# Self attention's heads in sets of four: four products side by side in one PSUM bank

## What is computed

```python
qkv = h @ w_qkv
q, k, v = jnp.split(qkv, 3, axis=-1)          # reshaped to (B, S, H, hd)
scores = jnp.einsum('bqhd,bkhd->bhqk', q, k) * hd ** (-0.5)
scores = jnp.where(causal, scores, jnp.finfo(scores.dtype).min)
attn = jax.nn.softmax(scores, axis=-1)
o = jnp.einsum('bhqk,bkhd->bqhd', attn, v).reshape(B, S, D)
x_resid = x + o @ w_o
```

## Time and profile before

| | us |
|---|---|
| median of three runs (3508.27 to 3514.3) | 3511.59 |
| profiled execution, its own time | 3526.84 |
| its span, first to last instruction | 3524.6 |
| self attention, from the first maximum tile to the last head's end | 593.0 |
| PE busy in the span | 2867.8 |
| DVE, ACT, POOL busy in the span | 2089.9, 1436.8, 1370.2 |

### The profile page before, as it was taken

One profiled execution on the slowest core, in us unless ns is written; L12 is line 12 of the kernel. 1 busy time (PEld: TensorE's weight loads), 2 busy tenths in 40 slices (PEclk: granted clock), 3 DMA queues, 4 the chain that ended last, 5 costly groups with the idle time before them and its releaser, 6 DMA issues. The chain is left out here.

```text
span 3524.6 us, 30222 instructions
## 1 busy us (share of the span) xinstructions
PE 2867.8 (81%) x8560; PEld 1248.7 (35%) x8560; DVE 2089.9 (59%) x2977; ACT 1436.8 (41%) x2168; POOL 1370.2 (39%) x1138
## 2 busy tenths in 40 slices
PE   5888988888775877999999829999478887779966
PEld 1232332333222543222222228888132332226522
DVE  1899999999995436444444230000339999932233
ACT  4566556655643322333333302221246555422233
POOL 2588788778774012000000140000437788720010
PEclk8999999999998978999999959999589999986688
DMA  1222022012200002100100224444221022000000
GB/s 62 94 96 93 26 96 102 32 71 96 79 18 18 1 14 90 28 19 20 26 18 19 69 97 142 179 180 142 79 96 63 35 96 96 0 18 0 0 7 24
DMA packets 67914, 215.28 MB, mean 61 GB/s; under 512 B 15517, under 2 KB 40361, under 8 KB 48697
## 3 DMA queue, kind: packets, MB, share of 16 engines
q1 hardware_dynamic: 61384, 181.12, 14.4%
q10 hardware_dynamic: 3312, 24.12, 2.0%
q0 software_dynamic: 3072, 8.39, 0.7%
HBM read 187.97 MB, written 25.43 MB: 61 GB/s over the span
## 5 line engine op out<-in xcount | busy, mean ns | idle before, releaser
L750 POOL TENSOR_TENSOR s_dbu<-s_dx,s_bc 128x512 f32<-128x512 f32 x768 | 975.0, 1275 | 313.3 <-DVE s_psum L490 312.3
L420 PE MATMUL s_psum<-s_hc,ident 128*128 128x512 f32 x1536 | 850.2, 638 | 209.9 <-DVE s_hc L506 209.1
L639 ACT ACTIVATE s_psum<-s_dt,s_a_neg 128x512 f32<-128x512 f32 x768 | 526.5, 690 | 631.0 <-DVE s_hc L506 630.2
L506 DVE TENSOR_TENSOR s_hc<-s_psum,s_bc 128x512 f32<-128x512 f32 x768 | 519.5, 677 | 0.9 <-issue 0.6
L420 PEld LDWEIGHTS s_psum<-s_hc,ident 128*128 128x128 f32 x1536 | 240.0, 190 | 764.4 <-DVE s_hc L506 686.0
L490 DVE TENSOR_TENSOR_SCAN s_psum<-s_psum,s_state,s_dbu 128x512 f32<-128x512 f32 x384 | 490.5, 1277 | 10.2 <-ACT s_psum L639 10.2
L490 DVE TENSOR_TENSOR_SCAN s_psum<-s_psum,s_dbu 128x512 f32<-128x512 f32 x384 | 468.5, 1220 | 12.8 <-ACT s_psum L639 9.9
L1329 DVE TENSOR_REDUCE s_umax<-s_banks 128x1 f32<-128x512 f32 (+3 forms) x384 | 210.3, 554 | 282.6 <-PE s_banks L1195 223.5
L1233 PE MATMUL s_banks<-s_probs,s_vs 128*17 128x512 f32 (+3 forms) x768 | 324.4, 512 | 35.6 <-ACT s_ot L1410 32.3
L1419 ACT ACTIVATE s_probs<-s_banks 128x512 f32<-128x512 f32 (+3 forms) x384 | 187.3, 489 | 395.7 <-PE s_banks L1219 295.5
L1780 ACT ACTIVATE s_hidden<-s_banks,s_w 128x256 f32<-128x256 f32 x184 | 77.1, 470 | 302.8 <-PE s_banks L1603 302.8
(11 more groups left out here) (249 smaller groups left out, 3626.0 us busy)
## 6 DMA issues: line engine op xcount, KB each, us to landing
s_bc<-fwd_rows SPq DMA_DIRECT2D x64, 1024.0 KB, 4.8
s_bc<-m_rows SPq DMA_DIRECT2D x32, 1024.0 KB, 4.7
s_w<-in_moe_w SPq DMA_DIRECT2D x23, 1028.0 KB, 7.3
s_w<-in_moe_w ACTq DMA_DIRECT2D x23, 1024.0 KB, 5.6
s_stack<-qk_parts SPq DMA_DIRECT2D x192, 64.0 KB, 2.1
qk_parts<-s_parts SPq DMA_DIRECT2D x48, 128.0 KB, 1.8
moe_in_rows<-s_zero SPq DMA_DIRECT2D x1, 5888.0 KB, 19.1
s_xs<-moe_in_rows SPq DMA_DIRECT2D x23, 256.0 KB, 6.0
```

The source lines that it names most:

```text
L420: pe.matmul(psum[:, SCANS + block_no % 2, :], consts["ident"][:], hc[:, unit % PRODUCTS, :], start=(n == 0), stop=(n == NS - 1)).then_inc( ...
L506: dve.tensor_tensor(hc[:, unit % PRODUCTS, :], psum[:, unit % SCANS, :], bc[:, 2 * n + 1, :], ALU.mult)\
L639: act.activation(psum[:, unit % SCANS, :], dt[:, g % 2, i // NS, :], ACT.Exp, scale=a_neg[CHUNKS[g][0]][:, i:i + 1]).then_inc(decay_ready, 1)
L750: pool.tensor_tensor(dbu[:, unit % TERMS, :], dx[:, g % 2, i // NS, :], bc[:, 2 * n, :], ALU.mult)\
```

## The change

Heads are handled in sets of four of one batch, eight sets `q`, with all loops written out.

- The value product has weights of 32 columns (`VW`: 16 channels, the ones column, 15 columns of zeros). The four heads of a set write partitions 0, 32, 64 and 96 onwards of one bank, one after another in PE's list (`mix_heads`), straight from `v`; the copy `vs` by POOL goes. One semaphore increment per four.
- Outputs and maxima are transposed per set: four 128x128 transposes per half (`turn_out`), one transpose of 32 columns (`turn_max`), one row split for 32 partitions, three row DMAs per set. `copy_out` copies 128 partitions. All transposes use bank 6.
- PE's order: per unit four weight tiles, each followed by a maximum tile of the next set, and a fifth maximum tile (`MAX_STEP`), then the four products of the unit before. Set q + 1's maxima are done in set q's units 0 to 9 and turned in unit 10. Weights have three banks (2, 3, 7), maxima two.
- `stack` becomes `stack_q` and `stack_k` with three slots of four heads of one batch. A set's 12 DMAs are 128 KB each, in rows of 1024 elements; three sets are loaded ahead, the next when the set three back has its last weights.
- The whole of `v`'s columns 16 to 31 is cleared, then the ones are written, and `stack_k`'s ones cover 3 x 12288 elements.

The diff, cut: of functions that are replaced only the new lines and what they keep are shown; `store_row` has the same four steps as before, on 32 partitions; `misc` numbers the users of bank 6 in order.

```diff
 PARTS = 3
 QPARTS, KPARTS = (0, 0, 0, 1, 1, 2), (0, 1, 2, 0, 1, 0)
 STACK = len(QPARTS) * HD
-VW = HD + 1
+VW = 32
+SLOTS = 3
+WEIGHT_BANKS = (2, 3, 7)
...
-        vs = s.sb("vs", [P, B * QT, HH, VW])
-        stack = s.sb("stack", [STACK + PARTS, HH, 2, T], BF16)
-        umax = s.sb("umax", [P, 2, 12])
-        row = s.sb("row", [QT, 2, PARTS, P], BF16)
-        row_rest = s.sb("row_rest", [QT, P])
-        probs = s.sb("probs", [P, 4, CH])
-        ot = s.sb("ot", [VW, 2, S])
-        rden = s.sb("rden", [P, 2, QT, 1])
+        stack_q = s.sb("stack_q", [STACK + PARTS, SLOTS, HH, S], BF16)
+        stack_k = s.sb("stack_k", [STACK + PARTS, SLOTS, HH, S], BF16)
+        umax = s.sb("umax", [P, 2, HH, QT])
+        late_max = s.sb("late_max", [P, 2, HH, QT // 2])
+        row = s.sb("row", [HH * QT, 2, PARTS, P], BF16)
+        row_rest = s.sb("row_rest", [HH * QT, P])
+        probs = s.sb("probs", [P, 2 * HH, CH])
+        ot = s.sb("ot", [P, 2, CH])
+        rden = s.sb("rden", [P, 2, QT // 2, HH, 1])
...
         NU = len(UNITS)
-        NN = HH * B
-        NTURN = H // HH
+        NSETS = H // HH * B
+        TILES = NU * HH
+        MAX_STEP = 5
...
             for stored in parts_stored:
                 sp.wait_ge(stored, NCH // 2 * STORES)
+            sp.wait_ge(made, 4)
+            def load_set(q):
+                g, b = q // B, q % B
+                if q >= SLOTS:
+                    sp.wait_ge(scored, (q - SLOTS + 1) * TILES)
+                for which, stack, order in ((0, stack_q, QPARTS), (1, stack_k, KPARTS)):
                     for r, part in enumerate(order):
+                        sp.dma_start(stack[r * HD:(r + 1) * HD, q % SLOTS, :, :],
+                                     qk_d[which, part, g * HH:(g + 1) * HH, :, b * S:(b + 1) * S]
+                                     .rearrange("h e t -> e h t")).then_inc(stack_ready[q % SLOTS], 16)
+            def store_rows(q):
+                sp.wait_ge(row_ready, q + 1)
+                for part in range(PARTS):
+                    sp.dma_start(stack_q[STACK + part:STACK + part + 1, q % SLOTS, :, :],
+                                 row[:, q % 2, part, :]).then_inc(row_stored[q % 2], 16)
+            for q in range(SLOTS):
+                load_set(q)
+            store_rows(0)
+            for q in range(NSETS):
+                if q + 1 < NSETS:
+                    store_rows(q + 1)
+                if q + SLOTS < NSETS:
+                    load_set(q + SLOTS)
         @block.tensor
         def _(pe):
...
             pe.wait_ge(split2, 4 + NCH * 4)
+            pe.wait_ge(made, 4)
+            def max_tile(q, k):
+                u, j = k // HH, k % HH
+                t, half = MAX_UNITS[u]
+                i = q * TILES + k
+                if k == 0:
+                    pe.wait_ge(stack_ready[q % SLOTS], (q // SLOTS + 1) * (12 * 16))
+                if i >= 2:
+                    pe.wait_ge(max_read, i - 1)
+                w = min((t + 1) * P - half * CH, CH)
+                bank = banks[:, i % 2, :]
+                mm = pe.matmul(bank[:, 0:w], stack_q[0:STACK, q % SLOTS, j, t * P:(t + 1) * P],
+                               stack_k[0:STACK, q % SLOTS, j, half * CH:half * CH + w], start=True, stop=True)
+                if t // 4 == half:
+                    mm = pe.matmul(bank[:, w - P:w], consts["identb"][:], lateb[:, 0, :], start=False,
+                                   stop=True, skip_group_check=True)
+                mm.then_inc(max_ready, 1)
+            def turn_max(q):
+                pe.wait_ge(maxed, q + 1)
+                if q:
+                    pe.wait_ge(misc_read, misc["max", q])
+                pe.transpose(banks[0:HH * QT, 6, 0:P], umax[:, q % 2, :, :].rearrange("p j t -> p (j t)"),
+                             consts["ident"][:]).then_inc(turned, 1)
+            def weight_tile(q, u, j):
+                t, half = UNITS[u]
+                i = q * TILES + u * HH + j
+                if u == 0 and j == 0:
+                    pe.wait_ge(row_stored[q % 2], (q // 2 + 1) * (PARTS * 16))
+                if i >= len(WEIGHT_BANKS):
+                    pe.wait_ge(exp_done, i - len(WEIGHT_BANKS) + 1)
+                q0 = max(t * P, half * CH)
+                w = (half + 1) * CH - q0
+                bank = banks[:, WEIGHT_BANKS[i % len(WEIGHT_BANKS)], :]
+                mm = pe.matmul(bank[:, 0:w], stack_k[:, q % SLOTS, j, t * P:(t + 1) * P],
+                               stack_q[:, q % SLOTS, j, q0:q0 + w], start=True, stop=True)
+                if t // 4 == half:
+                    mm = pe.matmul(bank[:, 0:P], consts["identb"][:], lateb[:, 1, :], start=False, stop=True,
+                                   skip_group_check=True)
+                mm.then_inc(scored, 1)
+            def mix_heads(q, u):
+                g, b = q // B, q % B
+                t, half = UNITS[u]
+                if q and t == 0:
+                    pe.wait_ge(ot_copied, 2 * (q - 1) + half + 1)
+                pe.wait_ge(exp_done, q * TILES + (u + 1) * HH)
+                w = (half + 1) * CH - max(t * P, half * CH)
+                for j in range(HH):
+                    mm = pe.matmul(banks[j * VW:(j + 1) * VW, 4 + half, CH - w:CH], v[:, b * QT + t, g * HH + j, :],
+                                   probs[:, u % 2 * HH + j, 0:w], start=(t == 0), stop=(t == 4 * half + 3))
+                mm.then_inc(pv_done, 1)
+            def turn_out(q, half):
+                pe.wait_ge(ot_copied, 2 * q + half + 1)
+                pe.wait_ge(misc_read, misc["out", q, half])
+                for t in range(QT // 2):
+                    mm = pe.transpose(banks[:, 6, t * P:(t + 1) * P], ot[:, half, t * P:(t + 1) * P], consts["ident"][:])
+                mm.then_inc(o_ready, 1)
+            for k in range(TILES):
+                max_tile(0, k)
+            turn_max(0)
+            for q in range(NSETS):
+                for u in range(NU):
+                    for j in range(HH):
+                        weight_tile(q, u, j)
+                        if q + 1 < NSETS and u * MAX_STEP + j < TILES:
+                            max_tile(q + 1, u * MAX_STEP + j)
+                    if q + 1 < NSETS and u * MAX_STEP + HH < TILES:
+                        max_tile(q + 1, u * MAX_STEP + HH)
+                    if u:
+                        mix_heads(q, u - 1)
+                    if q and u == 2:
+                        turn_out(q - 1, 1)
+                    if u == 7:
+                        turn_out(q, 0)
+                    if q + 1 < NSETS and u == 10:
+                        turn_max(q + 1)
+                mix_heads(q, NU - 1)
+            turn_out(NSETS - 1, 1)
+            pe.wait_ge(misc_read, len(misc))
...
         @block.vector
         def _(dve):
-            for sem in (max_read, row_ready, normed):
-                dve.sem_inc(sem, 1)
             dve.sem_inc(split2, 4)
             dve.sem_inc(out_free, 4)
-            dve.memset(v[:, :, :, HD:VW], 1.0).then_inc(made, 1)
-            dve.memset(stack[STACK:STACK + PARTS, :, 1, :], 1.0).then_inc(made, 1)
+            dve.memset(v[:, :, :, HD:VW], 0.0).then_inc(made, 1)
+            dve.wait_ge(made, 1)
+            dve.memset(v[:, :, :, HD:HD + 1], 1.0).then_inc(made, 1)
+            dve.memset(stack_k[STACK:STACK + PARTS, :, :, :], 1.0).then_inc(made, 1)
...
+            def maxima(q, k):
+                u, j = k // HH, k % HH
+                t, half = MAX_UNITS[u]
+                i = q * TILES + k
+                w = min((t + 1) * P - half * CH, CH)
+                to = umax[:, q % 2, j, t:t + 1] if half == 0 else late_max[:, q % 2, j, t - 4:t - 3]
+                dve.wait_ge(max_ready, i + 1)
+                dve.tensor_reduce(to, banks[:, i % 2, 0:w], AX.X, ALU.max).then_inc(max_read, 1)
+            def finish_max(q):
+                dve.wait_ge(max_read, (q + 1) * TILES)
+                dve.tensor_tensor(umax[:, q % 2, :, 4:8], umax[:, q % 2, :, 4:8], late_max[:, q % 2, :, :], ALU.max)\
+                   .then_inc(maxed, 1)
+            def store_row(q):
+                dve.wait_ge(turned, q + 1)
+                if q >= 2:
+                    dve.wait_ge(row_stored[q % 2], q // 2 * (PARTS * 16))
+                low = banks[0:HH * QT, 6, 0:P]
...
+            def norm_heads(q, half):
+                g, b = q // B, q % B
+                m = banks[:, 6, :].rearrange("p (t j e) -> p t j e", t=QT // 2, j=HH)
+                dve.wait_ge(o_ready, 2 * q + half + 1)
+                dve.reciprocal(rden[:, half], m[:, :, :, HD:HD + 1]).then_inc(rden_ready, 1)
+                dve.wait_ge(rden_ready, 2 * q + half + 1)
+                t0 = b * QT + half * QT // 2
+                dve.tensor_tensor(on[:, t0:t0 + QT // 2, g * HH:(g + 1) * HH, :], m[:, :, :, 0:HD],
+                                  rden[:, half].to_broadcast([P, QT // 2, HH, HD]), ALU.mult).then_inc(misc_read, 1)
+            for k in range(TILES):
+                maxima(0, k)
```

(63 more changed lines are left out.)

201 lines of the change are left out of this document (21 added, 180 removed).

## The result

The changed kernel takes 3292.68 us (median of 4 runs, 3291.57 to 3298.22), the kernel before beside it on the same chip 3510.43 us. The profiled execution takes 3291.57 us, its span is 3289.6.

What follows compares the result with a forecast made beforehand. TensorE was the bound, value products its largest part. (33.8 + 7 x 55.5 + 41) x 1.012 = 469 us for 593: 124 saved, less 7.8 setup, 2 loads, 8 clock: 106, median 3405 us; range 3305 to 3490.

Steps and rivals of the forecast that it cites:

- Products in four strips: Value products on TensorE: a group of four takes five stream lengths, 2.15 us plus 0.15 for loads; 21.2 us per set.
- a0 b0 a1 b1: Assumed TensorE order in a group: a and b are a product's two passes; b0 waits for a0, a1 may run beside b0.
- Rival B: Value products overlap fully, b0 not blocking a1: two streams per group, set 44, part 374, total 3310 us; chance 0.16.
- Rival A: Strips do not run side by side: eight passes in turn, set 65.6, part 551, total 3480 us; chance 0.20.
- The factor of 1.012: Correction to the laid-out part with heads: the layout gave 586 us for the kernel before's 593.0.
- Rivals C and D: C: TensorE's clock at its lower level throughout, 3621 us, chance 0.09. D: no net change, Rival A with strip drains, 0.05.
- Changes of mode: TensorE switching between bf16 tiles and value products: 12 per set instead of 48, 2.3 us for 9.1.
- Maxima: Five maximum tiles per unit, two DVE banks: TensorE newly waits for reduces, 0.92 us per full unit, some 6.5 per set.
- Row at the edge: TensorE idles 2.5 to 3 us at each of 7 set edges, waiting for the next set's maximum row.
- Prologue: Before the sets: 48 maximum tiles paced by DVE, 28 us, plus the uncovered row chain, 5.9: 33.8 us, previously 17.80.
- Setup: DVE's clearing of v and larger ones for stack_k, ahead of its first split: 7.8 us more, not covered.
- Loads: First set's 12 transfers of 128 KB instead of 64 KB before the first tile: 2 us more (0 to 6).

Runs made afterwards that it cites:

- the kernel with two strips: Against the changed kernel, the first two products of a group write the first strip, the last two the second: 3337.27 us, ratio 0.9516 to the kernel before.
- the first experiment: Against the changed kernel, all four products of a group write the first strip, so none run side by side: 3448.12 us, ratio 0.9826 to the kernel before.
- the spread kernel: Against the changed kernel, the four products keep their strips but stand apart, one after each head's weights and maxima: 3460.68 us, ratio 0.9860 to the kernel before.

## Why the prediction was wrong

**The bound of the kernel before** was read rightly: products with the values, on TensorE, were what could be gained.

**Products in four strips: the step that failed.** The text put it so: "TensorE starts matmuls in program order", so "b0 must wait for a0, a1 may run beside b0", five streams, 2.15 us and 0.15 for loads. Measured: two streams and 1.00 us. A product that waits for its own strip does not hold back one for another strip, as the kernel with two strips shows (1.85 us for 4 streams). The order a0 b0 a1 b1 was an inference from rows in which all matmuls used the same columns; they could not tell blocking from mere order. How the wait is resolved inside, by a queue for each strip or by an order other than I assumed, the traces leave open. The eight records of a group start as four and four, 0.45 us apart, and name no strip. Per set, the groups take 6 x 1.00 and, by the start differences of the narrower ones (0.78, 0.57 and 0.36 us for 384, 256 and 128 columns, twice each), 3.4 us for the other six: 9.4 in all, where 21.2 were set. That is 11.8 us per set, 94 us of the part.

The Trainium skill states both sides. "TensorEngine Tiling (Array Packing)", Key Properties, has tiles that work independently, and this case's group of 1.00 us agrees. "TensorE: Matmul & The Clock Gate", Part 3, has matmuls that start and end strictly in program order; the group with two strips disagrees, if its products reach TensorE in the order of the program, because there the third product did not wait for the second. The same Part 3 has 2.38 for three column strips; the four strips here gave 3.55.

**Rival B** was this case, with 0.16. It gave a group of 1.05, a set of 44 and a part of 374 us; measured are 1.00, 42.0 and 359.8. Its 3310 is 17 us above the result. **Rival A** was built as the first experiment: set 65.6, part 551 and 3480 forecast, 61.6, 517.4 and 3448 measured. Both were too long in the same direction. For A the mis-sized term is the clock: the layout gave 62.6 at full clock, I spread 0.93 over it, and 0.99 was granted. The factor of 1.012 and the last set's 52 carry the rest. **Rivals C and D** are excluded: the clock of the main stretch is 0.94, and changing strips costs nothing that can be seen (1.00 us for four products, 0.98 for one).

**Changes of mode.** A product alone takes 0.98 us for 0.86 of streams, and about 0.09 more stands before it in the spread kernel, where 0.19 per pair was set: the size holds. It was no lever: of 55 us of changes saved, 45 were eaten by waits for VectorE and ScalarE.

**Maxima.** 6.5 us of waits per set were forecast. From start to start it is 37 us in seven sets, 5.2 each, so the term holds. "ACT isn't late" nearly holds too: 10 us over all sets. **Row at the edge:** 2.5 to 3 us forecast, 2.7 measured. The clock behind it was set at 1 us per edge and measured 2.4. **Prologue:** 33.8 forecast, 35.0 measured. **ACT's pause** of 34 us went, as said.

**Setup:** 7.8 us forecast; VectorE's first split moved from 8.8 to 18.1 us behind the first matmul, 9.3. The zeros took 3.47 for my 4.3, but a gap of 2.62 us came before the last memset. **Loads:** 2 us forecast (0 to 6), 6.9 measured: 14.5 us from first issue to first tile for 7.6 (5.2 to 7.1 over all kernels with this load). I had taken the issue as the pace (0.49 a transfer), but the transfers themselves are slower. A set of four heads is 1.57 MB, which alone needs 14.3 us, 110 GB/s; before, half the bytes in a quarter of the packets (192 of 4 KB, now 768 of 2 KB) took 7.6. The time went with the bytes and not with the packets, though no run changes one alone. So the first maximum tile came 17 us later, not 10.

**The sum.** Part 469 forecast and 359.8 measured, 109 us more saved: seven sets of 42.0 for 55.5 are 95 us, the last set with 30.7 for 41 is 10, the factor of 1.012 is 5, and the prologue takes 1 back. The text gives 55.5 for a set of 53.8 at a clock of 0.93 without the working; the 41 us of weights, maxima and groups would by themselves grow by 3.1. Setup and loads took 16 us for 10. The 8 us put aside for the clock are already inside the measured part. 106 + 109 + 8 - 6 = 217, for 218.

## What to carry to other kernels

When a trace shows a resource used in one way only, order of starts is no evidence of blocking: keep the case of full overlap at more than a small chance, and price it first, because it is the largest. When the busiest engine gets much faster, look for what it will now wait for: here a short chain of about 6 us at each set's edge cost its own wait of 2.7 us and 2.4 us of clock. Moving it three units ahead, with the maxima spread evenly, gave 50 us of 3293. Idle time of the weight loads' queue is no measure of such a cost; the distance from start to start on TensorE is. Work that must be done before the first link of a chain (fills, constants) belongs on an engine that is idle later.

## What the runs showed of the hardware

- Four fp32 products in four strips of 32 columns: 1.00 us for 512 columns, against 3.55 on one strip and 0.98 for one product alone. Three products more cost 0.02 us.
- A product waiting for its strip does not delay one for another strip: 1.85 us for two and two, if they come in the program's order. Two products of one strip wrote the same PSUM addresses in all runs here, so whether the columns or the addresses made them wait is not separated.
- Eight weight loads of 32 columns in these groups: 0.16 us in all.
- TensorE's waits for the row between sets, seven in each kernel, and the granted clock: with 2.69 to 2.71 us it was at 0.50 at all seven, for 3.4 or 6.8 us; with 2.04 us (two strips) at three; with 1.11 us (spread products) and 0.77 us (one strip) at none. The length of a wait alone does not decide: in the kernel before, with 30 pauses of 1.1 to 1.4 us between products, the clock fell ten times.
- Twelve transfers of 128 KB from DRAM to 16 partitions each, in rows of 2 KB on one queue: 14.3 us.
- GpSimd wrote 3x12288 bf16 ones in 10.33 us and 128x4096 zeros in 3.51, VectorE in 10.30 and 3.47.
